# The quantised attention stage begins with the statistics of four tiles and two rounded weights; the rest is made in its first rounds

## The reference, cut to what matters

```python
def act_quant(x):                       # per row
    scale = 127.0 / clip(max(abs(x), -1), 1e-5)
    return clip(round(x * scale), -128, 127) / scale
def bit_linear(x, W):                   # weights rounded to -1, 0, 1
    s = clip(mean(abs(W)), 1e-5)
    return x @ (clip(round(W / s), -1, 1) * s).T
x = x + attention(layernorm(x), Wq, Wk, Wv, Wp)   # 16 heads of 16, every projection a bit_linear
```

## Time and profile before

| | before |
|---|---|
| median of 3 runs | 1777.76 us (1777.14 to 1778.35) |
| the profiled execution, its own time | 1782.12 us |
| its span in the trace | 1780.3 us |
| granted TensorE clock over the span | 0.861 |
| PE, DVE, ACT, POOL busy | 80%, 75%, 57%, 20% |

### The profile page before, as it was taken

How to read it: one execution, slowest core, us unless ns; L and a number is a source line. 1 busy time by engine, 2 the same in 40 slices (tenths; PEclk the granted TensorE clock), 3 DMA queues, 4 the chain that set the end, 5 groups by cost and what they waited for, 6 DMA issues and landing times. The chain is left out here.

```text
span 1780.3 us, 38229 instructions
## 1 busy us (share of the span) xinstructions
PE 1423.0 (80%) x13101; PEld 909.2 (51%) x13116; DVE 1342.5 (75%) x2547; ACT 1009.8 (57%) x1731; POOL 349.8 (20%) x509
## 2 busy tenths in 40 slices
PE   1777785899999999999997645973888699845992
PEld 0455553444444444444446545962666467634891
DVE  6888876688888888888886773548898556585774
ACT  1777763476766766666762432543677355454461
POOL 1122214100000000000000244652333200046241
PEclk9565655999999999999998767986999699958996
DMA  6950001133333333333320243533000000034335
GB/s 135 311 177 1 1 1 35 39 71 73 87 74 90 75 88 78 84 81 78 87 36 2 75 144 113 172 134 97 2 1 0 1 2 0 1 118 128 102 105 163
DMA packets 156618, 136.21 MB, mean 77 GB/s; under 512 B 73729, under 2 KB 137801, under 8 KB 156387
## 3 DMA queue, kind: packets, MB, share of 16 engines
q1 hardware_dynamic: 146627, 111.46, 24.7%
q0 software_dynamic: 7776, 21.28, 3.3%
q10 hardware_dynamic: 2112, 2.10, 0.4%
HBM read 66.85 MB, written 40.30 MB: 60 GB/s over the span
## 5 line engine op out<-in xcount | busy, mean ns | idle before, releaser
L2698 ACT ACTIVATE lat_Pb<-banks 125x896 f32<-125x896 f32 x384 | 328.4, 925 | 148.3 <-PE banks L2594 145.8
L2808 DVE TENSOR_TENSOR lat_dsum<-lat_dsum,lat_Pb 125x896 f32<-125x896 f32 x320 | 349.5, 1092 | 70.1 <-ACT lat_Pb L2698 62.5
L2572 PE MATMUL banks<-lat_Pb,lat_kv 125*64 125x448 f32 x1536 | 309.6, 545 | 0.0
L2594 PE MATMUL banks<-lat_Q,lat_kT 64*125 64x448 f16 x2304 | 256.8, 358 | 3.9 <-DVE lat_QT L2740 1.3
L2594 PEld LDWEIGHTS banks<-lat_Q,lat_kT 64*125 64x125 f16 x2304 | 141.1, 132 | 148.1 <-issue 66.2
L2572 PEld LDWEIGHTS banks<-lat_Pb,lat_kv 125*64 125x64 f32 x1536 | 101.7, 136 | 165.8 <-issue 157.9
L3103 POOL MEMSET moe_one<- 128x16 f32 (+1 forms) x2 | 0.2, 109 | 648.6 <-POOLq L259 648.6
L3152 POOL DMA_INDIRECT sent_outputs<-moe_yb,moe_yidx x98 | 95.7, 976 | 117.3 <-ACT moe_yb L3411 102.1
L3290 PE MATMUL banks<-moe_w2d,moe_gT 88*128 (+3 forms) x780 | 102.5, 282 | 17.6 <-DVE moe_gT L3629 13.6
L3617 DVE COPY moe_xTb<-banks 128x1024 f16<-128x1024 f16 x49 | 33.9, 691 | 80.3 <-PE banks L3257 80.3
L3290 PEld LDWEIGHTS banks<-moe_w2d,moe_gT 88*128 88x128 f16 (+1 forms) x780 | 77.0, 101 | 30.9 <-issue 19.2
(11 more groups left out here) (453 smaller groups left out, 3013.4 us busy)
## 6 DMA issues: line engine op xcount, KB each, us to landing
lat_Q<-lat_QT SPq DMA_DIRECT2D x128, 112.0 KB, 3.5
moe_xb<-sent_rows SPq DMA_DIRECT2D x49, 257.0 KB, 2.9
lat_raw<-in_ctx_dram SPq DMA_DIRECT2D x32, 375.0 KB
sent_rows<-zero SPq DMA_DIRECT2D x1, 7453.0 KB, 40.6
lat_rD<-lat_reciprocals SPq DMA_DIRECT2D x62, 112.0 KB, 2.8
moe_arena<-sent_outputs SPq DMA_DIRECT2D x12, 512.0 KB, 6.7
sent_rows<-zero SPq DMA_DIRECT2D x1, 5140.0 KB, 58.1
sent_outputs<-zero SPq DMA_DIRECT2D x1, 4096.0 KB, 42.0
```

Source lines behind the costliest of these rows:

```text
L2572: ins = nc.tensor.matmul(ps[u * DC:(u + 1) * DC, 6, 0:8 * T], kv[:, par, tt, :], Pb[:, tile_slot(tt, par), u, :], start=tt == 0, stop=tt = ...
L2594: ins = nc.tensor.matmul(ps[0:KP, n % 3 * 2 + q, 0:8 * T], kT[rows, par, 2 * pair + low, 0:KP], Q2[rows, par, w, 8 * u:8 * u + 8, :].rearr ...
L2698: nc.scalar.activation(Pb[:, slot:slot + 2, u, :], ps[0:KP, n % 3 * 2:n % 3 * 2 + 2, 0:8 * T], ACT.Exp, scale=1.0 / QSCALE).then_inc(exp_d ...
L2808: ins = nc.vector.tensor_tensor(dsum[:, par], dsum[:, par], Pb[:, tile_slot(tt, par)], ALU.add)
```

## The change

`row_stats` gets an argument `upto`, which the quantised stage sets to `FIRST_TILES = 4`; the other callers keep 16. With it the first block makes statistics, means, variances, roots and reciprocals of tiles 0 to 3 only, and it waits there for the first half of x only. The loop over weights becomes a function `quantise(then, m)`, which the first block calls for m = 0 and 1. The second block does the rest on DVE: `quantise(then, 2)` ahead of the rounds; in `body(-2)` the BATCH_NORM_STATS of tiles 4 to 7, the wait for the second half of x, and tiles 8 to 11; in `body(-1)` those of tiles 12 to 15, all twelve aggregates, the means and the variances; in `body(0)`, between `center` and `weight_sums`, the reciprocals and `quantise(then, 3)`. ACT makes the later square roots in `body(0)` ahead of its exponential. There are new waits: PE waits for the value weights before its first round and for the output weights in `body(1)`, and POOL waits for the later reciprocals in `body(1)`.

```diff
@@ row_stats
-            if load_x:
+            if upto < NT:
+                dve.wait_ge(k["x_in"][0], 64)
+                for i in range(upto):
+                    nc.vector.bn_stats(raw[:, i, :], x[:, i, :]).then_inc(own_bn, 1)
+            elif load_x:
...
-            dve.wait_ge(own_bn, NT)
-            for i in range(NT):
+            dve.wait_ge(own_bn, upto)
+            for i in range(upto):
                 s(nc.vector.bn_aggr(mv[:, i, :], raw[:, i, :]))
@@ quantised_weights
-            for m in range(4):
...
+            for m in range(2):
+                quantise(then, m)
             nc.vector.tensor_copy(ax[:, 1:2], sw[:, 3:4]).then_inc(dve_prepared, 1)
+
+        def quantise(then, m):
+            wm = wraw[:, :, m, :]
+            then(nc.vector.tensor_scalar(wm, wm, rsw[:, m:m + 1], MAGIC, ALU.mult, ALU.add))
+            then(nc.vector.tensor_scalar(wm, wm, MAGIC, 1.0, ALU.subtract, ALU.min))
...
@@ POOL body
+                    if isinstance(i, int) and i == 1:
+                        pool.wait_ge(late_rates, 1)
@@ ACT body
+                    if isinstance(i, int) and i == 0:
+                        act.wait_ge(late_var, 1)
+                        nc.scalar.activation(st["sd"][:, 0, FIRST_TILES:NT], st["var"][:, FIRST_TILES:NT],
+                                             ACT.Sqrt).then_inc(late_root, 1)
                     if live(i):
                         act.wait_ge(centered, i + 1)
                         nc.scalar.activation(E[:], E[:], ACT.Exp, scale=0.25).then_inc(exp_done, 1)
@@ PE
+                pe.wait_ge(values_quantised, 1)
                 if latent:
                     for i in range(-2, NT + 1):
+                        if i == 1:
+                            pe.wait_ge(outputs_quantised, 1)
                         body(i, i % 2)
@@ DVE
+                def statistics(first, last):
+                    for n in range(first, last):
+                        s(nc.vector.bn_stats(st["raw"][:, n, :], x[:, n, :]))
+
+                def later_variances():
+                    s.settle()
+                    for n in range(FIRST_TILES, NT):
+                        s(nc.vector.bn_aggr(st["mv"][:, n, :], st["raw"][:, n, :]))
+                    s.settle()
+                    s(nc.vector.tensor_copy(st["mean"][:, later], st["mv"][:, later, 0]))
+                    nc.vector.tensor_scalar(st["var"][:, later], st["mv"][:, later, 1], HEPS, None,
+                                            ALU.add).then_inc(late_var, 1)
+
+                def later_rates():
+                    dve.wait_ge(late_root, 1)
+                    then(nc.vector.reciprocal(st["r"][:, later], st["sd"][:, 0, later]))
+                    dve.sem_inc(late_rates, 1)
 
                 def body(i, par):
                     if live(i + 2):
                         normalise(i + 2, par)
                     if live(i + 1) and not causal:
                         heads(i + 1, (par + 1) % 2)
+                    if isinstance(i, int) and i == -2:
+                        statistics(FIRST_TILES, 8)
+                        dve.wait_ge(k["x_in"][1], 64)
+                        statistics(8, 12)
...
+                    if isinstance(i, int) and i == -1:
+                        statistics(12, NT)
+                        later_variances()
+                    if isinstance(i, int) and i == 0:
+                        later_rates()
+                        quantise(then, 3)
+                        dve.sem_inc(outputs_quantised, 1)
...
+                quantise(then, 2)
+                dve.sem_inc(values_quantised, 1)
                 over_tiles(dve, body, 2, s, STEPS[kind], tail=2 if bit else 1)
```

More of the change, by code:

```diff
@@ L241, in row_stats @@
 def row_stats(nc, ctx, name, k, double=False, load=None, zero=None, ready=None, sums=None,
-              act_first=None, act_last=None, buffers=None):
+              act_first=None, act_last=None, buffers=None, upto=NT):
     def sb(n, shape):
@@ L295, in _ @@
                     eight(n)
-            dve.wait_ge(own_bn, NT)
-            for i in range(NT):
+            dve.wait_ge(own_bn, upto)
+            for i in range(upto):
                 s(nc.vector.bn_aggr(mv[:, i, :], raw[:, i, :]))
             s.settle()
-            s(nc.vector.tensor_copy(st["mean"][:], mv[:, :, 0]))
-            nc.vector.tensor_scalar(var[:], mv[:, :, 1], HEPS, None, ALU.add).then_inc(var_made, 1)
+            s(nc.vector.tensor_copy(st["mean"][:, 0:upto], mv[:, 0:upto, 0]))
+            nc.vector.tensor_scalar(var[:, 0:upto], mv[:, 0:upto, 1], HEPS, None, ALU.add
+                                    ).then_inc(var_made, 1)
             dve.wait_ge(rooted, 1)
-            s(nc.vector.reciprocal(st["r"][:], sd[:, 0, :]))
+            s(nc.vector.reciprocal(st["r"][:, 0:upto], sd[:, 0, 0:upto]))
             if double:
@@ L325, in _ @@
             act.wait_ge(var_made, 1)
-            nc.scalar.activation(sd[:, 0, :], var[:], ACT.Sqrt).then_inc(rooted, 1)
+            nc.scalar.activation(sd[:, 0, 0:upto], var[:, 0:upto], ACT.Sqrt).then_inc(rooted, 1)
             if act_last:
@@ L1307, in self_attention @@
             own_weights = sem("dve_weights")
+            values_quantised, outputs_quantised = sem("value_weights_made"), sem("output_weights_made")
+            late_var, late_root, late_rates = (
+                sem("later_variances_made"), sem("later_roots_made"), sem("later_rates_made"))
             zc = sb("zc", [P, D])
@@ L1407, in quantised_weights @@
             then(nc.vector.reciprocal(rsw[:], sw[:]))
-            for m in range(4):
[L1409 to L1422, removed]
-            nc.vector.tensor_copy(ax[:, 1:2], sw[:, 3:4]).then_inc(dve_prepared, 1)
+            for m in range(2):
+                quantise(then, m)
+            nc.vector.tensor_copy(ax[:, 1:2], sw[:, 3:4]).then_inc(dve_prepared, 1)
+        def quantise(then, m):
+            wm = wraw[:, :, m, :]
+            then(nc.vector.tensor_scalar(wm, wm, rsw[:, m:m + 1], MAGIC, ALU.mult, ALU.add))
+            then(nc.vector.tensor_scalar(wm, wm, MAGIC, 1.0, ALU.subtract, ALU.min))
+            dst = wq[:, :, m * D:(m + 1) * D] if m < 3 else wo[:]
+            if m < 2:
+                for c in range(2):
+                    then(nc.vector.tensor_scalar(
+                        dst[:, c].rearrange("p (q a e) -> p q a e", a=2, q=2),
+                        in_halves(wm[:, c]), -1.0, None, ALU.max))
+            else:
+                then(nc.vector.tensor_scalar(dst, wm, -1.0, None, ALU.max))
+            if m < 3:
+                then(nc.vector.tensor_copy(
+                    swrow[:, 16 * m:16 * m + 16], sw[:, m:m + 1].broadcast_to([P, 16])))
         def weight_sums(pe):
@@ L1429, in self_attention @@
         st = row_stats(nc, ctx, f"{kind}_stats", k, double=rot, load=load_weights, zero=zero_buffers,
-                       ready=quantised_weights if bit else None, sums=weight_sums if bit else None)
+                       ready=quantised_weights if bit else None, sums=weight_sums if bit else None,
+                       upto=FIRST_TILES)
         with nc.Block() as block:
@@ L2056, in _ @@
                 hnorm = st["hnorm"] if rot else None
+                later = slice(FIRST_TILES, NT)
+                def statistics(first, last):
[13 more added lines that the diff above has]
+                    dve.sem_inc(late_rates, 1)
                 def body(i, par):
@@ L2085, in body @@
                         add_output(i - 1)
+                quantise(then, 2)
+                dve.sem_inc(values_quantised, 1)
                 over_tiles(dve, body, 2, s, STEPS[kind], tail=2 if bit else 1)
+FIRST_TILES = 4
 STEPS = {"bit": 25, "rot": 11, "causal": 2}
```

## The result

| | before | after |
|---|---|---|
| median, first comparison, 4 runs each | 1777.51 us (1777.14 to 1778.35) | 1768.36 us (1765.45 to 1771.94) |
| ratio, with its 95% interval | | 0.9946 [0.9934, 0.9958] |
| the profiled execution, its own time | 1782.12 us | 1771.94 us |
| its span | 1780.3 us | 1770.2 us |
| granted TensorE clock over the span | 0.861 | 0.867 |

The ratio makes 1777.51 x 0.0054 = 9.6 us, between 7.5 and 11.7. The forecast was 7.1. The direction was right. Most of what follows asks where the other 2.5 us come from.

The account below looks back on a forecast made before the run. The start was taken as bound by DVE's gapless first-block chain, on which all engines and the latent-weight DMAs wait. 7.84 - 0.75 = 7.1 us off 1777.76 gave 1770.7 us, range 1768.0 to 1774.0.

Parts of the forecast that it names:

- The first block: DVE before the barrier: removing two weights, twelve statistics and twelve aggregates saves 7.84 us; the wait for x costs 0.
- The clash with POOL: Second block's start: weight 2 takes turns with POOL, first normalisation 1.04 us later; 0.27 without clash, 1.43 with full exclusion.
- The statistics in the holes: Rounds body(-2) and body(-1): the moved statistics and aggregates fit DVE's waits, costing 0 and 0.1 us.
- The round of tile 0: First latent product's copy on ACT comes 0.75 us late against the shifted kernel, after the delayed center.
- ACT's path: Round of tile 0: square root, table load and exponential on ACT finish last, making the copy 0.75 us late.
- the latent weights: Their loads, issued 7.84 us earlier behind the barrier, keep their distance to PE; cost 0.
- this rival: Latent-weight DMAs become the bound, at worst the old 1777.8 us; sign: PE's DMA wait grows; chance 0.04.
- Weight 3 and the reciprocals: DVE after center in body(0): 1.2 us extra lateness, hidden before ACT's later need; cost 0, or 1.2 without cover.
- The steady rounds: Fifteen rounds keep their length, 14.47 us mean; the rival that they get slower, up to 1789.4 us, had chance 0.05.
- From the first round to the end: Everything behind the first rounds just shifts; three runs within 1.2 us taken to show that clock-grant shifts average out.

Follow-up runs that it names:

- E4: Changed kernel with its weights part alone, all sixteen statistics kept in the first block; 1777.47 us, ratio 1.0006 to the kernel before.
- E6: Changed kernel reordered: four statistics fill DVE's first hole, value weight rounded after the first normalisation; 1768.62 us, ratio 0.9951 to the kernel before.
- E8: Changed kernel with the edits of both E6 and E7; 1767.30 us, ratio 0.9951 to the kernel before.
- E7: Changed kernel with two of the eight latent-weight loads issued earlier, by ACT in the first block; 1769.61 us, ratio 0.9955 to the kernel before.
- E10: Kernel before, unedited, a second repeat for its trace in the slow session of E9; 1745 us from latent-product copy to end.
- E9: Kernel before, unedited, repeated for its trace; 1800.26 us timed in that session, 1742 us from latent-product copy to end.
- E1: Changed kernel again, no edit; 1771.47 us in 12 runs against 1776.99 in 25 of the kernel before, ratio 0.9970.
- E5: Changed kernel a third time, no edit; 1768.51 us in 6 runs against 1778.09 in 15 of the kernel before, ratio 0.9952.
- E2: Kernel before with the eight sums of absolute weights made four times, to shift everything later by 7.95 us; 1782.98 us, ratio 1.0041.
- E3: Changed kernel with its statistics part alone, all four weights rounded in the first block; 1771.29 us, ratio 0.9965 to the kernel before.

## Why the prediction was right or wrong

- **The first block.** 7.84 us forecast, 7.9 measured. The four statistics did not wait for x, and in the second block the ninth did not either. The cost of 0 was right in the changed kernel, but the reason was thin: the row of the old kernel proved only that x was in by 24.3, and E4 shows that it was in by 22.9, 1.4 us before that need.
- **The clash with POOL.** 1.04 us forecast between 0.27 and 1.43. Measured 2.61 - 1.58 = 1.03, with DVE's steps stretched to 0.65 and 0.72 and POOL's to 0.67. The stretched rows of before carried it. By the rule of the Trainium skill (SBUF — State Buffer, "Who interferes with whom") the second to start waits until the first is done. The trace agrees that both have waited here, but full turns would have made 1.43. E6 shows that it is the order alone: with statistics in that place it is 1.71 - 1.58 = 0.13.
- **The statistics in the holes.** 0 and 0.1 forecast. The eight took 2.69 beside POOL's 0.61 and 0.61, unstretched. Between the first normalisation and `center` nothing was lost: `center` ended 22.15 us behind the block's first row where it was 21.13, 1.0 later where 1.1 was forecast.
- **The round of tile 0.** 0.75 us forecast, 8.03 - 7.23 = 0.80 measured, and yet the step was wrong. I had ACT's path as the last, with PE 0.3 late. By E6 and E8 the load was the last in that trace, with ACT's path only 0.3 us before it. The sentence "I cost 0" of the latent weights is the failed one: from SP's first issue to PE's start behind the DMA the load took 51.17 - 29.30 = 21.87 us before, and 43.95 - 21.27 = 22.68 after. ACT's path was sized too large as well: its copy would have come 23.23 behind the block's first row (E7), 0.50 later than the 22.73 of before and not 0.75. The two errors cancelled, which is luck. The sign that I named for this rival did not show it: PE's wait for the DMA fell from 0.82 to 0.49, because PE itself came 1.1 us later. Nor is the 0.80 the same in each execution: the copy is 22.73, 22.65 and 22.10 behind the first row in the three traces of before (the first, E10, E9), and 23.53, 23.42 and 23.11 in the three of after (the first, E1, E5); in the third of each PE did not wait for the load. The means differ by 0.86.
- **Weight 3 and the reciprocals** were hidden, as forecast: DVE still waits 1.19 us for ACT one round later, where it waited 2.85. The three steps of weight 3 took 2.10 us beside POOL, where alone they took 1.42: the clash cost 0.7 and not 0.2, under that cover.
- **The steady rounds.** No change forecast, with 0.1 us a round as the sign of being wrong. They took 217.5 us where they took 216.9, 0.04 us a round. That rival did not come.
- **From the first round to the end.** The step that failed for the time is the sentence that three runs within 1.2 us mean that such shifts average out, and with it the lower end of the range. What the forecast took over unchanged behind these rounds differed by 2.9 us between the two first traces. Runs of one kernel spread over 8 us (E1: 1772.46 to 1780.69 for the kernel before). The three runs of before most likely lay close together by chance: three runs drawn from the 44 are that close in about one case of 17. The sign stood in my own table: the profiled execution was 4.4 us above the three, and I carried that over as a constant, so that the changed kernel's should have taken 1775.0; it took 1771.94. The shift itself is kept, as forecast: 7.23 us at the last place that the change touches, 7.2 us in the mean of all runs. The range of 1768.0 to 1774.0 was made for the mechanism, and held little room for a median of four runs, which by an estimate from the deviation of 2.5 varies by some 1.4 us. The 9.6 us of the first comparison and the 5.3 of E1 are both draws around 7.2. Where such differences come from is shown in part only: the 6 us of the rotary stage go with the clock granted to PE, but in the first two traces this stage gives 0.6 of the 2.9 us, and the experts, with clocks of 0.80 and 0.82, give 2.3. For these and the rest the clock is likely and not shown, and E9 and E10 have a stage that is longer without it.

## What to carry to other kernels

A stall that is worked around by filling holes is paid in the round where most chains meet, so look for every resource that ends last there within a microsecond; here ACT and the load were 0.3 apart, and removing either alone gave 0 to 0.3 of the 0.75 us that both gave. Work that looks like overhead can cover a load: moving the weights alone brought the barrier 1.4 us forward, since 1.6 of their 3.1 us became a wait for x, and moving them with the statistics brought it forward by their full time. And where PE's clock changes from run to run, take the spread from many runs before setting a range: three close ones prove nothing.

## What the runs showed that was not expected

The load of the latent weights is slower in the changed kernel, and one packet of the instruction queue falls into it; in E2, which has the rounds of before, none does. The views are the DMA queues from SP's first issue to just before PE's start, of after and of E2: packets, MB, share of 16 engines.

```profile
q1 hardware_dynamic: 5961, 5.59, 103.8%
q14 instruction: 1, 0.01, 0.2%
```
```profile
q1 hardware_dynamic: 5862, 5.14, 103.6%
```

From SP's first issue to PE's start behind the DMA it is 22.68 us after, 22.57 in E1, 22.66 in E6 and 22.95 in E3, which all have added instructions in the rounds; it is 21.87 before and 21.80 in E2, which have not. The times from issue to landing show the same without PE: the last two of the eight loads (`lat_wq`) took 13.5 us in the first trace of before and in E2, E4 and E10, and 13.3 in E9; they took 14.4 in after, E1, E3 and E6, and 14.2 in E5. So the load is slower in E5 too, where PE started 22.21 us after the first issue without waiting for the DMA.

The packet itself is not new. Each of these kernels has one, of 8 KB: in the kernel before it comes at 24.3 us, in E2 at 25.8 and in E4 at 26.8, when the load has not begun; in after it comes at 32.4, 11 us into the load, and takes 0.61 us. What goes with the slow load is its place. E4 has weights in the rounds but no statistics, and its load is fast, so the weights alone do not do it. Nor does x: in E3 the load begins at 24.47, behind the arrival of x (22.9 in E4), and it is the slowest. That the packet is the cause was not tried by itself: the statistics in the rounds came with it each time.

The other surprise is that one stage with identical instructions takes 212 or 218 us, with the granted clock at 0.89 or 0.84.
